# A two-layer gated cross-attention block: inverse deviations by GpSimd's power, row clearing and counts moved in the first layer, 8-bit integers as ScalarE's output in the feed-forward

## The reference

```python
x = x + tanh(g_xattn[0]) * L0_xattn(layernorm(x), ctx)
x = x + tanh(g_ffn[0])   * L0_ffn(layernorm(x))
x = x + tanh(g_xattn[1]) * L1_xattn(layernorm(x), ctx, mask)
x = x + tanh(g_ffn[1])   * L1_ffn(layernorm(x))
```

## Time and profile before

| what | value |
|---|---|
| median of three runs | 2155.1 us (2150.84 to 2159.89) |
| the profiled execution: its own time | 2150.62 us |
| its span | 2148.9 us, 1.7 less than its time |
| mean granted clock of PE | 0.954 of full speed |
| busy share of the span | PE 85%, DVE 74%, ACT 52%, POOL 42% |
| chain that ended last | PE 35%, DVE 30%, another core or an unknown queue 10%, issue 9%, DMA 7%, ACT 4%, POOL 4% |
| the scatters L1922 | 512, 984 ns each on the average |
| the maximum L793 | 128, 2293 ns each |

### The profile page before, as it was taken

One profiled execution on the slowest core, in us unless ns is written; L12 is line 12 of the kernel. 1 busy time (PEld: TensorE's weight loads), 2 busy tenths in 40 slices (PEclk: granted clock), 3 DMA queues, 4 the chain that ended last, 5 costly groups with the idle time before them and its releaser, 6 DMA issues.

```text
span 2148.9 us, 56605 instructions
## 1 busy us (share of the span) xinstructions
PE 1825.1 (85%) x20848; PEld 1451.8 (68%) x20848; DVE 1583.3 (74%) x6070; ACT 1117.6 (52%) x2299; POOL 900.0 (42%) x844
## 2 busy tenths in 40 slices
PE   5998888888889889746999978999999999968856
PEld 3777777777777777636888856676676667643334
DVE  5788888888888888772444447787887878778977
ACT  2555555555555555412222225666666666648877
POOL 1255555555555555574777750000000000005558
PEclk8999999999999999967999989999999999999988
DMA  9821111121111111045999951111111111102355
GB/s 234 217 80 56 53 51 48 48 68 53 41 36 43 43 42 38 22 138 127 225 210 219 208 102 40 46 39 45 40 41 43 39 46 39 31 24 108 127 204 188
DMA packets 184178, 187.98 MB, mean 87 GB/s; under 512 B 37042, under 2 KB 166613, under 8 KB 181856
## 3 DMA queue, kind: packets, MB, share of 16 engines
q1 hardware_dynamic: 136384, 142.69, 21.5%
q0 software_dynamic: 47520, 41.67, 10.5%
HBM read 103.72 MB, written 140.77 MB: 114 GB/s over the span
## 4 chain that ended last, share of the span: by engine, by line
PE 35%; DVE 30%; another core or an unknown queue 10%; issue 9%; DMA 7%; ACT 4%; POOL 4%; SPq 1%; POOLq 0%; ACTq 0%; DVEq 0%
DVE mt L793 8%; DMA accumulator<-ye,tid 6%; PE bank L513 5%; PE tiles L363 4%; PE bank L393 4%; PE tiles L346 3%; PE bank L476 3%; PE bank L465 2%; PE bank L445 2%; DVE hmax L1617 2%; POOL accumulator L1407 2%; PE bank L536 2%; DVE qm L805 2%; DVE newton L880 2%
## 5 line engine op out<-in xcount | busy, mean ns | idle before, releaser
L1922 POOL DMA_INDIRECT expert_rows<-pay,idx x512 | 503.7, 984 | 374.8 <-issue 107.8
L793 DVE TENSOR_REDUCE mt<-tiles 128x16 f32<-128x2048 f32 x128 | 293.5, 2293 | 49.6 <-PE tiles L346 37.1
L1936 POOL TENSOR_TENSOR res<-res,bias 128x256 f32<-128x256 f32 x64 | 46.3, 724 | 573.4 <-ACT xn L637 573.4
L594 ACT ACTIVATE pt<-tiles 128x2048 f32<-128x2048 f32 x128 | 241.6, 1887 | 44.3 <-PE tiles L363 44.1
L1407 POOL DMA_INDIRECT accumulator<-ye,tid x128 | 198.5, 1551 | 93.7 <-DMA accumulator<-ye,tid 34.8
L617 ACT ACTIVATE qkp<-bank,kb,keep 128x128 f32<-128x128 f32 x500 | 205.1, 475 | 0.0
L363 PE MATMUL tiles<-qm,qkp 32*128 32x128 f32 x4096 | 152.6, 286 | 40.1 <-DVE mt L793 36.9
L363 PEld LDWEIGHTS tiles<-qm,qkp 32*128 32x128 f32 x4096 | 127.8, 188 | 69.3 <-DVE mt L793 50.3
L430 PE MATMUL bank<-xt,w_q 128*128 128x128 f32 x1024 | 167.1, 287 | 3.2 <-issue 2.2
L393 PE MATMUL bank<-pt,vx 128*32 128x128 f32 x4096 | 160.2, 277 | 11.1 <-issue 9.1
L430 PE MATMUL bank<-cxax,w_k 128*128 128x128 f32 x1000 | 156.8, 279 | 0.6 <-issue 0.6
(11 more groups left out here) (263 smaller groups left out, 4175.0 us busy)
## 6 DMA issues: line engine op xcount, KB each, us to landing
expert_rows<-zt POOLq DMA_DIRECT2D x16, 1032.0 KB
xr<-expert_rows SPq DMA_DIRECT2D x64, 258.0 KB
cxax<-in_ctx SPq DMA_DIRECT2D x128, 128.0 KB
cxax<-accumulator SPq DMA_DIRECT2D x128, 128.0 KB, 2.2
hidden_away<-h_ring SPq DMA_DIRECT2D x8, 1536.0 KB, 5.0
res<-in_x SPq DMA_DIRECT2D x64, 128.0 KB
accumulator<-xa SPq DMA_DIRECT2D x64, 128.0 KB
accumulator<-zt SPq DMA_DIRECT2D x64, 128.0 KB
```

The costliest lines, as they stand in the source:

```text
L594: nc.scalar.activation(pt[r % 2][:, :, :], tiles[:, :, :], ACT.Exp).then_inc(sem(sm("exp_done")), 1)
L793: nc.vector.tensor_reduce(mt[:, :].rearrange("p (i n c) -> p i n c", i=RT, n=2 * KC)[:, :, :, 0], tiles[:, :, :].rearrange("p i (n k) -> p ...
L1922: G.indirect_dma_start(out=xe[:, :], out_offset=bass.IndirectOffsetOnAxis(ap=idx[r][:, n:n + 1], axis=0), in_=pay[r][:, :], in_offset=None ...
```

## The change

- `inverses` of DVE keeps three steps: variance plus epsilon, a wait, nmr. Between them POOL computes rstd = var ^ (-0.5) with one instruction (`inverse_roots`), which waits for the first step and for ACT's last reads of rstd. This holds for both layers.
- POOL's queue in the first layer: two row clearing steps ahead (a step is two DMAs), then per slot the power for the next slot, one row clearing step (in step 8 the accumulators' instead), the eight scatters. A clearing step waits for the step two before it.
- POOL's queue in the second layer: the power, then the bias addition.
- In the first layer PE's counts move from the slot's end to right behind the scores of the next slot, and from bank 6 to bank 5; the v projection comes after heads to tokens and uses bank 4; the waits for the banks are moved accordingly. DVE takes the maximum ahead of the dispatching, and the routing steps are spread otherwise.
- Second layer, DVE: one step of the inverse deviations, the key shift, the last step.
- Feed-forward: ACT writes int8 instead of fp32 plus RND. In pass 0 POOL's two instructions become one copy int8 to bf16 (DVE's two for chunk 0 likewise). In pass 1 POOL's clip, ACT's `integer` and DVE's `floored` and `capped` go; DVE makes three copies int8 to bf16 per chunk, each for two blocks; the bring of a chunk waits for ACT alone.

```diff
...
-NORM_STEPS = 13
+NORM_STEPS = 3
...
+ZEROED_AHEAD = 2
...
-        wait(pe, sm("silu_done"), b - 4)
-        wait(pe, sm("qm_done"), b - 1)
+        pe.wait_ge(sem(sm("v_out")), b + 1)
...
+      wait(pe, sm("qk_out"), 2 * b)
...
-        pe.wait_ge(sem(sm("v_out")), b + 1)
-      else:
-        wait(pe, sm("qk_out"), 2 * b)
+        wait(pe, sm("pos_done"), b - 5)
...
-        wait(pe, sm("qk_out"), 2 * b)
+        wait(pe, sm("silu_done"), b - 4)
+        wait(pe, sm("qm_done"), b - 1)
...
-      bk = bank[5 if L == 0 else 4]
...
-        last = nc.tensor.matmul(bk[:, 0:D], cx[r][:, c, :], w_v[:, c, :],
+        last = nc.tensor.matmul(bank[4][:, 0:D], cx[r][:, c, :], w_v[:, c, :],
...
-      wait(pe, sm("pos_done"), b)
+      pe.wait_ge(sem(sm("en_out")), b + 1)
...
       pe.wait_ge(sem(sm("sel_done")), b + 1)
-      pe.wait_ge(sem(sm("en_out")), ahead(b, 2))
-      nc.tensor.matmul(bank[6][:, 256:256 + E], strict_tri[:, :], sel[r % 2][:, :], start=True, stop=True)
-      nc.tensor.matmul(bank[6][:, 256 + E:256 + 2 * E], ones_e[:, :], sel[r % 2][:, :], start=True,
+      pe.wait_ge(sem(sm("qk_out")), 2 * ahead(b, 6))
+      nc.tensor.matmul(bank[5][:, 0:E], strict_tri[:, :], sel[r % 2][:, :], start=True, stop=True)
+      nc.tensor.matmul(bank[5][:, E:2 * E], ones_e[:, :], sel[r % 2][:, :], start=True,
                stop=True).then_inc(sem(sm("counts_done")), 1)
...
     def body(stage):
-      g, f, m, k, o, w, v = (stage(lag) for lag in range(-1, 6))
+      g, f, m, k, o, w, v, u = (stage(lag) for lag in range(-1, 7))
       scores(m)
       if L == 0:
+        moe_counts(u)
+        heads_to_tokens(o)
         project_v(f)
-        heads_to_tokens(o)
         moe_down(v)
...
-        moe_counts(v)
...
-      nc.scalar.copy(vx[r][:, :, 0:DH], bank[5 if L == 0 else 4][:, 0:D].rearrange("p (h d) -> p h d", h=H)
+      nc.scalar.copy(vx[r][:, :, 0:DH], bank[4][:, 0:D].rearrange("p (h d) -> p h d", h=H)
...
-      st.need()
-      st.mark(V.tensor_scalar(root[:, :].bitcast(i32), var[:, :].bitcast(i32), 1, None, ALU.arith_shift_right))
-      yield
-      st.need()
-      st.mark(V.tensor_scalar(root[:, :].bitcast(i32), root[:, :].bitcast(i32), -1.0, float(0x5f3759df), ALU.mult, ALU.add))
-      for step in range(3):
-        yield
-        st.need()
-        st.mark(V.scalar_tensor_tensor(newton[:, :], root[:, :], -0.5, root[:, :], ALU.mult, ALU.mult))
-        yield
-        st.need()
-        st.mark(V.tensor_tensor(newton[:, :], newton[:, :], var[:, :], ALU.mult))
-        yield
-        st.need()
-        if step == 2:
-
-          wait(dve, sm("xn1_done"), min(s1, NB))
-          wait(dve, sm("xn2_done"), s1 - PAIR[L])
-        st.mark(V.scalar_tensor_tensor((rstd if step == 2 else root)[:, :], newton[:, :], 1.5, root[:, :],
-                         ALU.add, ALU.mult))
-      yield
-      st.need()
+      dve.wait_ge(sem(sm("rstd_step")), NORM_STEPS * s1 + 2)
+      st.k += 1
...
-      st.mark(V.tensor_tensor(place[:, :], bank[6][:, 256:256 + E], count[:, :], ALU.add))
-      V.tensor_tensor(count[:, :], bank[6][:, 256 + E:256 + 2 * E], count[:, :], ALU.add).then_inc(sem(sm("pos_done")), 1)
+      st.mark(V.tensor_tensor(place[:, :], bank[5][:, 0:E], count[:, :], ALU.add))
+      V.tensor_tensor(count[:, :], bank[5][:, E:2 * E], count[:, :], ALU.add).then_inc(sem(sm("pos_done")), 1)
...
+        maximum(m)
...
-        maximum(m)
...
           next(ahead_of_time)
-        routing(3)
+        routing(1)
         first_stats(n)
...
         shifted(m)
-        routing(5)
+        routing(8)
         residual(y)
...
         variances(n, y)
-        norming(5)
-        routing(1)
-        norming(2)
-        routing(1)
-        norming(2)
         routing(1)
         norming(1)
+        routing(1)
         silu(w)
-        norming(2)
         silu_up(w)
...
-        norming(11)
+        norming(1)
...
-        norming(2)
+        norming(1)
...
-      nc.scalar.activation(xq_f[c % 2][:, :], big[:, c * (TPC * D):(c + 1) * (TPC * D)], ACT.Copy,
-                 bias=RND, scale=scl[:, 1:2]).then_inc(sem("xq_rounded"), 1)
+      nc.scalar.activation(xq_i[c % 2], big[:, c * (TPC * D):(c + 1) * (TPC * D)], ACT.Copy,
+                 scale=scl[:, 1:2]).then_inc(sem("xq_rounded"), 1)
...
-    def clip_tokens(c):
-      if not c:
-        return
-      pool.wait_ge(sem("xq_rounded"), c + 1)
-      nc.gpsimd.tensor_scalar(xq_f[c % 2][:, :], xq_f[c % 2][:, :], RND + QMAX, RND - QMAX - 1.0, ALU.min, ALU.max
-                  ).then_inc(sem("xq_clipped"), 1)
-
...
-      pool.wait_ge(sem("xq_clipped"), c)
+      pool.wait_ge(sem("xq_rounded"), c + 1)
...
-      nc.gpsimd.tensor_scalar(xq_b[c % 2][:, :, :].rearrange("p t d -> p (t d)"), xq_f[c % 2][:, :], -RND, None, ALU.add
-                  ).then_inc(sem("xq_done"), 1)
-
-    def body(stage):
-      clip_tokens(stage(0))
-      convert(stage(0))
-    ffn_chunks(body, NC_, 0)
+      nc.gpsimd.tensor_copy(xq_b[c % 2][:, :, :].rearrange("p t d -> p (t d)"), xq_i[c % 2]).then_inc(sem("xq_done"), 1)
+
+    ffn_chunks(lambda stage: convert(stage(0)), NC_, 0)
...
-    V.tensor_scalar(xq_f[0][:, :], xq_f[0][:, :], RND + QMAX, RND - QMAX - 1.0, ALU.min, ALU.max).then_inc(sem("first_capped"), 1)
-    dve.wait_ge(sem("first_capped"), 1)
-    V.tensor_scalar(xq_b[0][:, :, :].rearrange("p t d -> p (t d)"), xq_f[0][:, :], -RND, None, ALU.add
-            ).then_inc(sem("xq_done"), 1)
+    V.tensor_copy(xq_b[0][:, :, :].rearrange("p t d -> p (t d)"), xq_i[0]).then_inc(sem("xq_done"), 1)
...
-      nc.scalar.activation(slot_of(k)[:, i, :], slot_of(k)[:, i, :], ACT.Copy, bias=RND, scale=s_guq[:, i:i + 1]
+      if i % 2 == 0:
+        wait(act, "f_whole", IC // 2 * (k - 2) + i // 2 + 1)
+      nc.scalar.activation(h_i[k % 2][:, i, :], slot_of(k)[:, i, :], ACT.Copy, scale=s_guq[:, i:i + 1]
...
-    def integer(k):
-      if k is None:
-        return
-      act.wait_ge(sem("f_clipped"), k + 1)
-      wait(act, "f_down_done", TPC * (k - 1))
-      nc.scalar.activation(f_q[k % 2][:, IC - 2:IC, :], slot_of(k)[:, IC - 2:IC, :], ACT.Copy, bias=-RND
-                 ).then_inc(sem("f_last_out"), 1)
-
...
-      scaled(stage(0), 0)
-      scaled(stage(0), 1)
-      integer(stage(1))
-      for i in range(2, IC):
+      for i in range(IC):
...
-    ffn_chunks(body, NC_, 1)
+    ffn_chunks(body, NC_, 0)
...
-    def clip(k):
-      if k is None:
-        return
-      pool.wait_ge(sem("f_rounded"), IC * (k + 1))
-      h = slot_of(k)[:, IC - 2:IC, :]
-      nc.gpsimd.tensor_scalar(h, h, RND + QMAX, RND - QMAX - 1.0, ALU.min, ALU.max).then_inc(sem("f_clipped"), 1)
-
...
-      clip(stage(1))
...
-        residual(stage(2), t)
-    ffn_chunks(body, NC_, 2)
+        residual(stage(0), t)
+    ffn_chunks(body, NC_, 0)
...
-    def floored(k, p):
+    def whole(k, p):
...
-      V.tensor_scalar(f_q[k % 2][:, 2 * p:2 * p + 2, :], slot_of(k)[:, 2 * p:2 * p + 2, :], RND - QMAX - 1.0, -RND,
-              ALU.max, ALU.add).then_inc(sem("f_floored"), 1)
-
-    def capped(k):
-
-      if k is None:
-        return
-      dve.wait_ge(sem("f_floored"), 2 * (k + 1))
-      q = f_q[k % 2][:, 0:IC - 2, :]
-      V.tensor_scalar(q, q, QMAX, None, ALU.min).then_inc(sem("f_first_out"), 1)
+      V.tensor_copy(f_q[k % 2][:, 2 * p:2 * p + 2, :], h_i[k % 2][:, 2 * p:2 * p + 2, :]).then_inc(sem("f_whole"), 1)
...
-      capped(stage(1))
-      rescaled(stage(2), 1)
-      rescaled(stage(2), 2)
-      rescaled(stage(2), 3)
-      floored(stage(0), 0)
+      whole(stage(0), 0)
...
-      floored(stage(0), 1)
-    ffn_chunks(body, NC_, 2)
+      rescaled(stage(1), 1)
+      whole(stage(0), 1)
+      rescaled(stage(1), 2)
+      rescaled(stage(1), 3)
+      whole(stage(0), 2)
+    ffn_chunks(body, NC_, 1)
...
-      pe.wait_ge(sem("f_first_out"), k + 1)
-      pe.wait_ge(sem("f_last_out"), k + 1)
+      pe.wait_ge(sem("f_whole"), IC // 2 * (k + 1))
...
-      sp.wait_ge(sem("f_first_out"), k + 1)
-      sp.wait_ge(sem("f_last_out"), k + 1)
+      sp.wait_ge(sem("f_rounded"), IC * (k + 1))
...
-    for n in range(8):
-      for h in range(HALVES):
-
-        wait(pool, f"xe_zero{h}", 16 * n)
-        G.dma_start(xe_v[n, h], zt[:, h, :].unsqueeze(1).broadcast_to([P, E // 8, ROW])).then_inc(sem(f"xe_zero{h}"), 16)
-    for h in range(HALVES):
-      pool.wait_ge(sem(f"xe_zero{h}"), 16 * 8)
-    for n in range(2):
-      G.dma_start(acc[n][T:T + HALVES * P, :].rearrange("(n p) d -> p n d", p=P), zt[:, :, 0:D]
-            ).then_inc(sem(f"xe_zero{n}"), 16)
+    def inverse_roots(eng, L, s):
+
+      if s >= NB + PAIR[L]:
+        return
+      eng.wait_ge(sem(f"rstd_step_{L}"), NORM_STEPS * s + 1)
+      wait(eng, f"xn1_done_{L}", min(s, NB))
+      wait(eng, f"xn2_done_{L}", s - PAIR[L])
+      G.tensor_tensor(rstd[:, :], var[:, :], minus_half[:, :], ALU.pow).then_inc(sem(f"rstd_step_{L}"), 1)
+
+    def zero_rows(n):
+
+      if n in range(8):
+        for h in range(HALVES):
```

(28 more changed lines are left out.)

12 lines of the change are left out of this document (8 added, 4 removed).

## The result

The changed kernel took 2249.2 us (median of 4 runs, 2244.0 to 2276.0) beside 2154.5 us of the kernel before: ratio 1.046, 95% interval 1.038 to 1.055. The forecast was 2126 us. The profiled execution has a span of 2243.0 us, 94.1 more than before.

What follows compares the result with a forecast made beforehand. Attention slots were taken as bound by loops of waits through several engines, pass 1 by ACT with POOL nearly full. From 2155.1 us, -29 - 3 + 17 - 1 - 13 = -29 gave 2126 us; range 2085 to 2190, likeliest case 2110 to 2145.

Steps and rivals of the forecast that it cites:

- part 2: First layer: POOL's power ahead of the scatters makes them run back to back, maximum later; +0.3 us per slot, +17 us.
- the row between them: First layer: profiled slot with 1.57 us of idle DVE before the maximum, taken between 0.84 and 2.58; 0.73 us more.
- rival B: First layer: four or more scatters in one run hold the scores back; +1.3 us per slot, 2185 us; chance 0.26.
- a break at the fourth scatter: First layer, POOL's queue: the fourth scatter must still see the slot's values, so the run pauses after the third.
- the row of the run of three: First layer: profiled slot with 2.58 us of idle DVE after a third scatter in a row; upper price +1.3 per slot, +76 us.
- Part 1: Inverse deviations: one POOL power replaces eleven DVE instructions per slot; second layer -29 us, bare chains -3 us.
- Part 3: Row clearing: the same 16 DMAs move from one block into slots; between -5 and +10 us, taken as nothing.
- Part 4: 8-bit feed-forward: pass 0 -1 us; pass 1 from 5.13 to 4.25 us per chunk, -13 us.
- Rival D: Pass 1: casts and additions exclude each other, 5.0 us per chunk, 2137 us; chance 0.12.
- Rival C: Second layer: POOL's power takes over 2.5 us and the gain there is gone, 2155 us; chance 0.10.
- Rival A: First layer: scatters bunch harmlessly, the maximum is not late; -0.5 us per slot, 2080 us; chance 0.18.

Runs made afterwards that it cites:

- e8: Changed kernel with the first layer's inverse deviations back on DVE in 13 steps, on a chip where the kernel before takes 2172.2 us: 2109.2 us, ratio 0.971.

## Why the prediction was wrong

- **The step that failed** is part 2, "the row between them, 1.57 us of idle time: 0.73 more, less the 0.4, +0.3 per slot, +17 us". The mechanism named was the one that happened, rival B, and even its upper price (+1.3 per slot, +76) was half of the measured +2.7 (slots of 16.5 us, from 13.8) and +153 us. Three things were missed. First, the prediction priced the maximum alone, and its lateness grew by only 1.55 us on the average. ACT's copies L662 (of the values' result) and L629 (v) have 89 and 55 us of "remote" idle time before them in the first layer, from 0 and 9. Something was given back, as forecast, ahead of the `at` copy (116 us, from 184), but it did not shorten the slot. Second, it counted on a break at the fourth scatter, a few sentences after saying that the fourth's condition had come by then; the values had been seen, and the fifth scatter went out as well. Third, it had no term for PE itself, which was busy 50 us longer, at a granted clock of 0.89 in place of 0.95. The row nearest to the size was in the prediction: 7.05 us of idle ACT behind seven scatters. It was put under a rival. The kernel before has one run of five or more scatters without a break in its first slots and three at the layer's end; the changed kernel has over thirty, all through the layer.
- The choice of the middle row rested on that break alone. With the row of the run of three, 2.58 us, the forecast would have been "slower", 2185 us, and still 64 too low.
- **Part 1** held: the power takes 0.71 us (0.7 forecast) and is hidden. The second layer gained 50 us and not 30. The slot's floor is 9.27 us, not 9.35: it lost 0.58 us, the 0.51 before the masks and a little more, 36 us in all. Another 5 went in its first slots, which makes 41 us from the first to the last maximum. The rest, 9 us, is at the layer's ends, where the forecast had 1.
- **Part 3** held: nothing shows (e8 keeps it and has ratio 0.971). The place of the counts, which the prediction put at nothing, costs nothing in e8 either.
- **Part 4**: pass 0 as forecast (1.1). Pass 1 gained 8.2 and not 13. The term mis-sized is the cast: 1.06 us beside POOL's additions, where 0.69 alone and some stretching had been taken; the chunk is 4.64 us behind the first, 4.73 in the mean, for 4.25. Rival D said 5.0. The Trainium skill, SBUF - State Buffer, section "SBUF: two separate sides", describes the port pair as a lock held for the whole instruction. The trace agrees: the ends of casts and additions never come closer than 0.55 and 0.58 us. Rival D had the mechanism right and its price too high, because it added full durations (0.69 and 0.72), of which a part overlaps. The section has the lock for some DVE operations only, and no view shows of which kind the cast is.
- **Rival C** did not come up. **Rival A** is what a prompt chip does: nothing is late, 11.4 us per slot. Neither the prediction nor its rivals could tell the two kinds of chip apart, as all its rows are from one.
